# A graph-network kernel on one Trainium2 core: the far rows of a tile pair get a landing buffer of their own

## The reference

```python
h = maximum(layernorm(x), 0)
x = x + L0(h)          # h = h @ W_enc.T + b_enc, then 2 message layers, then W_out
h = maximum(layernorm(x), 0)
x = x + L1(h)          # 3 layers: h = mean_of_neighbours(h) @ Wl.T + bl + h @ Wr.T, relu between
# one message layer of L0:
m   = relu(concat([h[row], h[col]]) @ msg_W1.T + msg_b1) @ msg_W2.T + msg_b2
agg = segment_sum(m, col)
h   = layer_norm(h + concat([h, agg]) @ upd_W.T + upd_b) * ln_g + ln_b
```

## Time and profile before

| | us |
|---|---|
| median of 3 timed runs | 3269.17 (3268.67 to 3272.48) |
| the profiled execution | 3254.39 |
| its span | 3252.6 |
| message layer 0, first half, about | 634 to 920 |
| message layer 0, second half, about | 920 to 1262 |
| message layer 1, first half, about | 1366 to 1653 |
| message layer 1, second half, about | 1653 to 2000 |

### The profile page before, as it was taken

One profiled execution on the slowest core, in us unless ns is written; L12 is line 12 of the kernel. 1 busy time (PEld: TensorE's weight loads), 2 busy tenths in 40 slices (PEclk: granted clock), 3 DMA queues, 4 the chain that ended last, 5 costly groups with the idle time before them and its releaser, 6 DMA issues.

```text
span 3252.6 us, 214630 instructions
## 1 busy us (share of the span) xinstructions
PE 2864.9 (88%) x88633; PEld 2657.9 (82%) x88633; DVE 2278.5 (70%) x4258; ACT 1694.1 (52%) x3386; POOL 737.7 (23%) x940
## 2 busy tenths in 40 slices
PE   4666665699999998799999998699999889998999
PEld 3555454599989998699989997689999889998999
DVE  8999999777767776677767776599999842224222
ACT  1433333577767776777767775668778620001000
POOL 2211223600011115500011114534444601100110
PEclk7777777899999999799999999699999999999999
DMA  4000000566666763366666665045555569995998
GB/s 75 7 6 6 6 5 5 167 182 184 185 169 186 189 187 91 115 186 186 185 173 185 183 183 135 1 151 184 187 185 184 162 208 296 295 293 173 302 305 271
DMA packets 365972, 518.83 MB, mean 160 GB/s; under 512 B 152480, under 2 KB 275910, under 8 KB 365896
## 3 DMA queue, kind: packets, MB, share of 16 engines
q1 hardware_dynamic: 352557, 498.96, 50.8%
q0 software_dynamic: 4000, 8.20, 2.4%
q10 hardware_dynamic: 9338, 10.73, 1.1%
HBM read 408.98 MB, written 108.72 MB: 159 GB/s over the span
## 4 chain that ended last, share of the span: by engine, by line
PE 70%; DVE 12%; issue 8%; DMA 3%; ACT 2%; POOL 2%; DVEq 0%; SPq 0%; ACTq 0%; POOLq 0%
PE psum L1403 19%; PE psum L1637 17%; PE psum L1421 9%; PE psum L1407 9%; PE psum L1622 5%; PE psum L1602 3%; PE psum L701 2%; DMA tabf<-in_x 1%; DVE arena L1674 1%; DMA arena<-rows_far,ovcur 1%; PE psum L2156 1%; DVE Hf L940 1%; PE psum L698 1%; DVE AGGf L985 1%; DVE Hf L1079 1%
## 5 line engine op out<-in xcount | busy, mean ns | idle before, releaser
L1403 PE MATMUL psum<-tabf,arena 125*32 125x128 f16 x40256 | 1091.3, 220 | 36.0 <-issue 16.2
L1403 PEld LDWEIGHTS psum<-tabf,arena 125*32 125x32 f16 x40256 | 949.2, 98 | 101.3 <-issue 54.8
L1407 PE MATMUL psum<-arena 96*32 96x128 f16 x20928 | 1027.5, 221 | 1.3 <-issue 1.3
L1454 ACT ACTIVATE arena<-psum 128x512 f32<-128x512 f32 x1300 | 775.1, 596 | 342.4 <-PE psum L1407 341.5
L1407 PEld LDWEIGHTS psum<-arena 96*32 96x32 f16 x20928 | 692.2, 95 | 1.4 <-issue 1.4
L1637 PE MATMUL psum<-tabf,arena 125*125 125x256 f16 x5000 | 562.3, 274 | 4.2 <-DVE tabf L2198 4.2
L1421 PE MATMUL psum<-arena 128*32 128x129 f32 x10400 | 565.6, 277 | 0.1
L1637 PEld LDWEIGHTS psum<-tabf,arena 125*125 125x125 f16 x5000 | 553.9, 138 | 5.0 <-issue 5.0
L1664 ACT CAST arena<-psum 125x500 f16<-125x500 f32 x625 | 354.0, 579 | 95.7 <-PE psum L1602 35.7
L1622 PE MATMUL psum<-tabf,arena 125*125 125x256 f16 x2500 | 379.9, 275 | 0.3 <-ACT arena L1664 0.3
L1359 POOL DMA_INDIRECT arena<-rows_far,ovcur x50 | 93.6, 1871 | 980.9 <-PE psum L1407 980.9
(11 more groups left out here) (325 smaller groups left out, 4234.8 us busy)
## 6 DMA issues: line engine op xcount, KB each, us to landing
arena<-cells_kept SPq DMA_DIRECT2D x200, 787.5 KB, 4.7
cells_kept<-arena SPq DMA_DIRECT2D x625, 126.0 KB, 1.7
arena<-slots_turned_from SPq DMA_DIRECT2D x152, 384.0 KB
tabf<-slots_turned_from SPq DMA_DIRECT2D x150, 384.0 KB, 4.0
arena<-slots_turned_from SPq DMA_DIRECT2D x50, 512.0 KB
tabf<-slots_turned_from SPq DMA_DIRECT2D x50, 512.0 KB
arena<-slots_turned_to SPq DMA_DIRECT2D x152, 96.0 KB
tabf<-slots_turned_to SPq DMA_DIRECT2D x150, 96.0 KB, 4.3
```

The costliest lines, as they stand in the source:

```text
L1403: pe.matmul(psCell[b][q:q + GW, g * D:(g + 1) * D], fr, rows, start=g == 0 and p == 0, stop=False, tile_position=(0, q), skip_group_check= ...
L1407: m = pe.matmul(psCell[b][q:q + GW, g * D:(g + 1) * D], toB[part][:, here + q:here + q + GW], cur[:, part, g, :], start=g == 0 and 4 * k + ...
L1454: act.activation(msgs[:, SLOT[pos], :, 0:D], psCell[SLOT[pos]].rearrange("p (c d) -> p c d", d=D), ACT.Relu).then_inc(f_msg, 1)
```

## The change

In the message layers the indirect DMA lands in a new tile `ovin`, of the same shape as `ovrows`. The request for a pair (`ask`) is issued one pair earlier, the first one of a layer ahead of the loop. In each turn GpSimd waits for the landing in `ovin`, copies the next index column, waits on `f_gat` for TensorE's last gather of the pair before, copies `ovin` to `ovrows` (128 x 256 f16) by `tensor_copy`, waits for that copy, adds 2 to `f_far`, and issues the request for the next pair. `f_ovi` now counts index copies and row copies. One more request a layer is made, for the index column behind the last pair, and its landing is awaited behind the loop. TensorE's, VectorE's, ScalarE's and SyncE's streams are as before.

```diff
@@ -312,6 +312,7 @@
         toE = [carve([128, n, RG, GW]) for n in SPAN]
         cur = carve([STACKED, 2, RG, D], F16)
         ovrows = carve([128, CP, D], F16)
+        ovin = carve([128, CP, D], F16)
         carve = carver(arena[:, STAGE_WORDS:], arena_words - STAGE_WORDS)
         slist = [[None, None], [None, None]]
         for n in range(2):
@@ -1348,28 +1349,34 @@
             if l == 0:
                 hold(pool, "pool", o_move, 48 * RG)
 
+            steps = l * (1 + 2 * PAIRED)
+
             def next_index(t):
 
                 at = slice(t, t + 1) if isinstance(t, int) else bass.ds(t, 1)
                 pool.tensor_copy(ovcur[:, 0:1], ovidx[:, at]).then_inc(f_ovi, 1)
 
-            def far_rows(t):
-
-                hold(pool, "pool", f_ovi, t + (l * (PAIRED + 1) + 1))
-                pool.indirect_dma_start(ovrows.rearrange("p c d -> p (c d)"), None, far_dram,
+            def ask(step):
+
+                hold(pool, "pool", f_ovi, step)
+                pool.indirect_dma_start(ovin.rearrange("p c d -> p (c d)"), None, far_dram,
                                         bass.IndirectOffsetOnAxis(ap=ovcur[:, 0:1], axis=0)).then_inc(f_over, 16)
 
             kk = 2 * l + 1
             if l:
-                hold(pool, "pool", f_ovi, l * (PAIRED + 1))
+                hold(pool, "pool", f_ovi, steps)
             next_index(0)
             hold(pool, "pool", f_table, 32 * NB_LOOPS * (l + 1))
+            ask(steps + 1)
             with pool.Fori(0, PAIRED) as i:
+                hold(pool, "pool", f_over, i * 16 + (l * (PAIRED + 1) + 1) * 16)
+                next_index(i + 1)
                 hold(pool, "pool", f_gat, i * (2 * VISIT[1]) + visit_done(-1, kk, VISIT[1] - 1, 2))
-                far_rows(i)
-                pool.wait_ge(f_over, i * 16 + (l * PAIRED + 1) * 16)
+                pool.tensor_copy(ovrows, ovin).then_inc(f_ovi, 1)
+                hold(pool, "pool", f_ovi, i * 2 + (steps + 3))
                 pool.sem_inc(f_far, 2)
-                next_index(i + 1)
+                ask(i * 2 + (steps + 3))
+            hold(pool, "pool", f_over, (l + 1) * (PAIRED + 1) * 16)
 
         def cells_pe(pe, l):
             for h in range(2):
@@ -1575,7 +1582,7 @@
                 pool.tensor_copy(ovto[:], regroup[:, 1, SPARE_J, 0:NT, SPARE]).then_inc(l_clear, 1)
                 hold(pool, "pool", s_tab, (l + 1) * NB_LOOPS)
                 own_slots(slice(0, 1), 0)
-            hold(pool, "pool", l_ovi if l else f_ovi, (l if l else L0) * (PAIRED + 1))
+            hold(pool, "pool", l_ovi if l else f_ovi, l * (PAIRED + 1) if l else L0 * (1 + 2 * PAIRED))
             next_index(0)
             hold(pool, "pool", h_rows, 32 * NB_LOOPS * (l + 1))
             with pool.Fori(0, PAIRED) as i:
```

## The result

The changed kernel takes 3290.6 us (median of 4, 3289.56 to 3299.31) against 3268.92 before (median of 4): 1.0076 times as long, interval 1.0062 to 1.0089. That is 21.7 us slower. The forecast was 3263.6, in a range up to 3272.

What follows compares the result with a forecast made beforehand. TensorE's own work plus its waits was taken to bound the message layers. Removing 5.5 us of far-row waits, with all replacement costs 0, gave 3254.39 - 5.5 = 3248.9 profiled, scaled to 3263.6 us timed; range 3252 to 3272.

Steps and rivals of the forecast that it cites:

- the 0.41 us worked out: GpSimd's new copy of 128 x 256 f16: its time with nothing beside it, from copies of the linear layers.
- 0.19: Microseconds VectorE's comparison would lose beside GpSimd's copy, scaled by length from 0.07 for 96 elements; counted as 0.
- the 0.9 us that were free: VectorE's comparisons before TensorE's fourth visit: they may be held up 0.9 us a pair for nothing.
- VectorE is held: Rival: copy and request hold VectorE's second comparison beyond 0.9 us, TensorE stands at even tiles' fourth visit; 3294 us, chance 0.10.
- the wait was covered: Rival: another wait right behind f_far, so nothing won; 3269 us, chance 0.13 shared with the doubled tenth.
- The request follows the copy: GpSimd's loop: request at about 1100.1 to 1101.2, landing 5 to 7 us later, around 1107, before it is needed.
- All of this: 0: Moved request, wait for f_over, index copy, two added requests and last landing together cost nothing.
- The 5.5 us: TensorE's weight-load waits on the far rows in message layers' second halves, all to go; bounds 4.2 and 7.0 us.
- The even tiles' tenth: Rival: even tiles' extra 0.10 us at the first scatter, as the request ends, vanishes (3258.6, chance 0.10) or doubles (3268.7).
- both its cases: Even tiles' 0.10 us lost: 5 us more won, chance 0.10; doubled: 5 given back, chance 0.13 shared with a covered wait.
- Later landings in the timed runs: Rival: landings 0.3 us later each make waits some 15 us; gain 8 to 20 us, 3249 to 3261, chance 0.23.

Runs made afterwards that it cites:

- e7: Changed kernel with two landing buffers in turn, the next pair's request first and the copy and raise of f_far behind it: 3261.55 us, 0.9991 times the kernel before.
- e3: Changed kernel without requests in the loop, only the first pair's far rows fetched, the copy kept: 3243.1 us, 0.9907 times the kernel before.
- e5: The kernel before, unedited, profiled a second time: 3268.12 us timed (1.0010), profiled execution 3270.25 us.
- e2: Changed kernel with the request held until TensorE's fourth gather of the even tile, some 3 us later, the copy unmoved: 3304.82 us, 1.0096 times the kernel before.
- e9: Changed kernel with each request for only the first 32 of the 128 rows: 3293.19 us, 1.0086 times the kernel before.
- e11: Changed kernel with the indirect request replaced by a plain DMA of the same size issued by GpSimd: 3236.59 us, 0.9902 times the kernel before.
- e12: Changed kernel with the indirect request replaced by a plain DMA of the same size issued from SyncE's queue: 3237.95 us, 0.9906 times the kernel before.
- e1: Changed kernel with GpSimd's loop cut so its jump back stands behind the index copy, same instruction order: 3292.93 us, 1.0063 times the kernel before.
- e4: The kernel before with GpSimd's loop cut so its jump back stands right behind the request, no copy: 3272.18 us, 1.0004 times the kernel before.

## Why the prediction was wrong

**What held.** The waits on the far rows are all gone. The request starts where it was expected: 1.97 us behind VectorE's first comparison, 1100.5 on the prediction's scale, for which it said 1100.1 to 1101.2. The copy takes the 0.41 us worked out where it meets no comparison (e7), and 0.88 beside VectorE's first one. VectorE's second comparison became 0.15 us longer (1.42 for 1.27 in the earlier trace rows), where the prediction had 0.19, far inside the 0.9 us that were free. That 0.19 was partly luck: its yardstick in the earlier trace rows, the comparison of 2224.53, had itself run beside the copy. e3 shows that the copy costs TensorE nothing. The rival "VectorE is held" is refuted, and so is "the wait was covered".

**The step that failed** is the one that begins with "The request follows the copy" and ends with "All of this: 0". The request's landing was costed and its start was not. It now starts 1.97 us behind the start of VectorE's first comparison (1052.65 - 1050.68) instead of 0.90 (1099.44 - 1098.54 in the earlier trace rows), at the end of VectorE's comparison rather than in it, and each one stops TensorE for about 1.07 us. The sum that should have stood there: even tiles go from 7.14 and 7.23 to 7.66 and 7.72, so by medians 25 x 0.52 + 25 x 0.49 = 25 us, 24.2 for the 48 even tiles among the 98. The 98 tiles themselves give 702.8 - 682.2 = 20.6 and the timed runs 21.7. The missing 3.6 lie in four tiles of e5 that were longer than their like: two even tiles of layer 1 by 0.7 each, and the first odd tile of each half (8.04 and 9.30, against 7.46 and 7.84 in the changed kernel).

The gain was mis-sized as well. The 5.5 us were the waits of the first profile; in e5, whose time is that of the timed runs, weight loads waited 1.6 us and matmuls 1.0. With 2.6 us at most to win, the forecast was some 3 us too low even before the request's price.

**The sign of it was in the rows.** "The even tiles' tenth" was this stop at its smallest: 0.11 us, just when the request ends, in even tiles alone, with no semaphore near. The prediction gave it as a rival, but took its size (0.10) as the bound of both its cases. The row bounded nothing: the price at another place had no row there, and this should have widened the range upwards.

**One execution is one execution.** The first profile was of the kind with small stops (662.6 us for the 98 tiles), the second with large ones (682.2), and the difference of 19.6, less 4 us by which the first took longer between the two layers' far matmuls (1258.4 to 1662.1, against 1267.3 to 1666.9), accounts for the 14.8 us by which the timed runs stood above the first. That the timed runs had large stops is inferred from their times, since only profiled executions show stops. "Later landings in the timed runs" explained the same 14.8 us and was wrong by the second profile: it was as long as the timed runs, and its waits for landings were smaller, 1.6 us of weight loads. Why one execution has stops of 0.1 and another of 0.57 was not settled.

**What the stop is.** Shown: it follows the indirect request and no other part (e2, e3, e7), 0.35 us behind its start; it does not depend on the rows asked for (e9); a plain DMA of the same size from either queue has none (e11, e12); its size changes with the place of the request. Requests of 0.97 us that start as a comparison ends cost their tile 1.07 us, those of 1.42 and 1.88 us beside a comparison cost 0.95 and 0.57. Duration alone does not set the price: requests of about 1.0 us cost 1.2 to 1.4 us at the place of e2, and those of 1.88 us cost 0.1 in the first profile.

Not shown: through what TensorE's instructions are held. The Trainium skill, page "SBUF — State Buffer", section "SBUF: two separate sides", says that GpSimd cannot write its descriptors while VectorE holds the port pair in an operation of a two-port mode. Whether the comparison is one no run here shows, but the requests of 1.88 us beside a comparison and 0.97 without one agree. A request that is itself slowed might press less on TensorE at a time. That last link is an argument, not a measurement, and it is not the whole of it: in e5 TensorE's first gap, behind the block of 1049.42, falls while the comparison still runs (1048.84 + 1.27 = 1050.11).

The Trainium skill, page "Runtime: NRT & Kernel Launch", section "Instruction fetch mechanics", says that a jump out of the pages an engine holds leaves it waiting for instructions. Moving GpSimd's jump (e1, e4) changed nothing. The trace of the changed kernel goes further. On its page the instruction queues are

```profile
q8 instruction: 38, 0.62, 0.1%
q14 instruction: 38, 0.31, 0.0%
```

and between 940 and 1265 us, where 22 requests start and every even tile has its stop, all the packets are

```profile
q1 hardware_dynamic: 33711, 55.59, 58.9%
q0 software_dynamic: 736, 1.51, 4.5%
```

None is in an instruction queue, so the stops are not waits for instructions that these queues bring.

## What to carry to other kernels

When an edit moves an asynchronous request off a wait, cost its start as well as its landing. What the request did here to the busiest engine in the microsecond behind it outweighed the wait. A small periodic loss without a semaphore, in step with some other engine's instruction, is a price whose size elsewhere is unknown, and the range must say so. Where the profiled execution and the timed runs stand further apart than the effect forecast, profile the kernel before once more before building on its rows.

## What was not expected of the hardware

An indirect DMA issued by GpSimd held up TensorE's stream of small matmuls by 0.1 to 1.4 us in these loops, where no semaphore stood, and the requests were worth 29 us in the kernel before and 50 in the changed one; a plain DMA of the same size was free (653.3 and 653.2 us for the 98 tiles, 652.7 with no request). Whether the 75 indirect requests of the linear layers cost TensorE anything was not looked at. Two requests 1.27 us apart made a stop of 2.4 us, behind which the granted clock was 0.50 for over 3 us; the 50 added requests cost 143 us where single stops would have cost 53.
